# First attention of a two-layer graph network: where the halves of a finished unit are added, on VectorE or on GpSimd

## The reference, cut to what matters

```python
wh = (x @ weight).reshape(n, NHEADS, OUT_FEATURES)
awh_i = (wh * linear_i).sum(axis=2)
awh_j = (wh * linear_j).sum(axis=2)
e = leaky_relu(awh_i[:, None, :] + awh_j[None, :, :], negative_slope=0.2)
e = e + ((1.0 - adj) * NEG_INF)[:, :, None]
a = softmax(e, axis=1)
out = einsum('ijh,jhf->ihf', a, wh)
```

## Time and profile before

| | us |
|---|---|
| median of 3 runs (4261.85 to 4263.58) | 4261.97 |
| the profiled execution, its device time | 4264.08 |
| its span, first to last instruction | 4260.6 |
| gat, from about 495 to 1493 us of the span | 998 |
| in gat: PE busy / DVE busy / ACT busy / POOL busy | 960.0 / 979.1 / 948.6 / 5.6 |

### The profile page before, as it was taken

One profiled execution on the slowest core, in us unless ns is written; L12 is line 12 of the kernel. 1 busy time (PEld: TensorE's weight loads), 2 busy tenths in 40 slices (PEclk: granted clock), 3 DMA queues, 4 the chain that ended last, 5 costly groups with the idle time before them and its releaser, 6 DMA issues. The chain is left out here.

```text
span 4260.6 us, 104547 instructions
## 1 busy us (share of the span) xinstructions
PE 3773.0 (89%) x42884; PEld 2512.9 (59%) x42884; DVE 3499.7 (82%) x6039; ACT 3344.7 (79%) x4233; POOL 439.5 (10%) x635
## 2 busy tenths in 40 slices
PE   7981399999999969919999999999999999999977
PEld 4540399999999924405555555555555555555533
DVE  6655699999999977638888888888888888888734
ACT  3433699999999822209999999999999999999932
POOL 1211100000000000020120201201112011120000
PEclk9995699999999979959999999999999999999989
DMA  9988855555554377662453534444445354353133
GB/s 347 392 287 210 242 175 170 184 188 189 189 188 164 121 206 238 209 174 71 116 138 90 142 95 119 133 101 131 107 108 138 93 142 109 95 143 93 45 111 138
DMA packets 364121, 674.35 MB, mean 158 GB/s; under 512 B 79584, under 2 KB 239408, under 8 KB 326784
## 3 DMA queue, kind: packets, MB, share of 16 engines
q1 hardware_dynamic: 296448, 574.83, 45.3%
q0 software_dynamic: 24064, 84.37, 6.5%
q10 hardware_dynamic: 43136, 8.53, 1.0%
HBM read 524.43 MB, written 143.20 MB: 157 GB/s over the span
## 5 line engine op out<-in xcount | busy, mean ns | idle before, releaser
L1230 DVE CUSTOM_DVE_ANT_0 m_junk<-m_rough,m_rows 128x1024 bf16<-128x1024 f32 x1024 | 1253.5, 1224 | 287.8 <-PE m_rough L1097 226.3
L1179 ACT ACTIVATE m_scores<-m_strip 128x1024 f32<-128x1024 fp8e4 x1024 | 1052.3, 1028 | 102.4 <-POOL m_strip L1028 37.9
L1193 ACT ACTIVATE m_whole<-m_scores 128x1024 int32<-128x1024 f32 x1024 | 1038.0, 1014 | 35.9 <-PE m_scores L1130 25.5
L630 PE MATMUL g_acc<-g_vals,g_pos 128*128 128x130 f16 x8192 | 956.4, 218 | 48.6 <-DVE g_neg L585 48.6
L547 ACT ACTIVATE g_step<-g_arow,k_steep 128x512 fp8e4<-128x512 f32 x1536 | 948.6, 707 | 40.2 <-DVE g_pos L578 37.2
L630 PE MATMUL g_acc<-g_vals,g_neg 128*128 128x130 f16 x8192 | 955.8, 221 | 0.0
L1111 PE MATMUL m_acc<-m_v,m_halves 128*128 128x129 f16 (+1 forms) x16384 | 897.1, 208 | 45.2 <-ACT m_got L1156 45.2
L1111 PEld LDWEIGHTS m_acc<-m_v,m_halves 128*128 128x128 f16 x16384 | 751.0, 98 | 279.8 <-issue 186.5
L630 PEld LDWEIGHTS g_acc<-g_vals,g_pos 128*128 128x128 fp8e4 x8192 | 801.9, 98 | 59.5 <-DVE g_neg L585 37.1
L1125 PE MATMUL m_scores<-m_qA,m_kA 128*128 128x512 f16 x2048 | 780.7, 381 | 5.7 <-ACT m_scores L1179 5.6
L630 PEld LDWEIGHTS g_acc<-g_vals,g_neg 128*128 128x128 fp8e4 x8192 | 784.9, 96 | 0.0
(11 more groups left out here) (161 smaller groups left out, 3005.2 us busy)
## 6 DMA issues: line engine op xcount, KB each, us to landing
g_vals<-scr_gat_v SPq DMA_DIRECT2D x128, 1040.0 KB, 5.1
m_v<-scr_v SPq DMA_DIRECT2D x64, 1032.0 KB, 7.9
a_stage<-in_adj SPq DMA_DIRECT2D x64, 1024.0 KB, 9.3
m_kA<-scr_k_hi SPq DMA_DIRECT2D x128, 512.0 KB, 6.2
scr_row_mask<-a_rowm SPq DMA_DIRECT2D x64, 512.0 KB, 7.6
m_kB<-scr_k_lo SPq DMA_DIRECT2D x64, 512.0 KB, 5.4
m_rows<-scr_row_mask POOLq DMA_DIRECT2D x64, 512.0 KB, 7.3
scr_gat_v<-a_early POOLq DMA_DIRECT2D x32, 520.0 KB, 6.9
```

What stands on the lines that cost most here:

```text
L630: mm = pe.matmul(acc[:, b, it, lo:hi], edges[:, n % RING, t, rows], vals[:, b, 4 * j + t, lo:hi], start=j == 0 and t == 0 and lo == 0, sto ...
L1179: nc.scalar.activation(scores[:, n % 2], strip[:, 2 * st:2 * st + 2, :].rearrange("p t i -> p (t i)"), ACT.Copy, bias=-BIG, scale=BIG / ED ...
L1193: nc.scalar.activation(whole[:, st % 2], scores[:, st % 2], ACT.Exp, scale=0.125).then_inc(exped, 1)
L1230: nc.vector.tensor_tensor_reduce(out=junk[:, n % 2], in0=rough[:].rearrange("p a m -> p (a m)"), in1=rows[:, n % TC, n // TC * WIDE:(n // ...
```

## The change

VectorE keeps only line 592 of `evacuate`. The three additions move to GpSimd, which now runs a function `join(u)` for each unit: it waits for `evac`, adds the halves (`part`, which raises the new semaphore `parted`), waits for its own `parted`, and adds `num` and `k.den`. VectorE may overwrite `scaled` for unit u only when GpSimd has read it for unit u - 1: one new wait, for `parted`, ahead of line 592. GpSimd waits for its own `den_made` before it overwrites `part`. The stage ends when GpSimd's last DMA has landed and its last `k.den` is written.

```diff
-        chain, evac, num_ready, passed = (s.sem(n) for n in ("chain", "evac", "num_ready", "passed"))
+        evac, parted, den_made, num_ready, passed = (s.sem(n) for n in ("evac", "parted", "den_made", "num_ready", "passed"))
...
                 dve.wait_ge(multiplied, QUADS * (u + 1))
+                if u > 0:
+                    dve.wait_ge(parted, u)
                 nc.vector.tensor_tensor(scaled[:], acc[:, b, :, 0:2 * VG].rearrange("p q (z v) -> p q z v", z=2),
                                         k.row_factors[:, c * TC:(c + 1) * TC, h, :].unsqueeze(3).to_broadcast([P, TC, 2, VG]),
                                         ALU.mult).then_inc(evac, 1)
-                dve.wait_ge(evac, u + 1)
-                link(nc.vector.tensor_tensor(part[:], scaled[:, :, :, 0:F + 1], scaled[:, :, :, F + 1:VG], ALU.add))
-                if h == 0 and c >= 2:
-                    dve.wait_ge(num_out[c % 2], 16 * (c // 2))
-                link(nc.vector.tensor_tensor(num[:, c % 2, :, h, :], part[:, :, 0, 0:F], part[:, :, 1, 0:F], ALU.add))
-                if h == H - 1:
-                    dve.sem_inc(num_ready, 1)
-                nc.vector.tensor_tensor(k.den[:, c * TC:(c + 1) * TC, h:h + 1], part[:, :, 0, F:F + 1], part[:, :, 1, F:F + 1], ALU.add)
...
         def _(pool):
+            def join(u):
+                c, h = u // H, u % H
+                pool.wait_ge(evac, u + 1)
+                if u > 0:
+                    pool.wait_ge(den_made, u)
+                nc.gpsimd.tensor_tensor(part[:], scaled[:, :, :, 0:F + 1], scaled[:, :, :, F + 1:VG], ALU.add).then_inc(parted, 1)
+                pool.wait_ge(parted, u + 1)
+                if h == 0 and c >= 2:
+                    pool.wait_ge(num_out[c % 2], 16 * (c // 2))
+                nc.gpsimd.tensor_tensor(num[:, c % 2, :, h, :], part[:, :, 0, 0:F], part[:, :, 1, 0:F], ALU.add).then_inc(num_ready, 1)
+                nc.gpsimd.tensor_tensor(k.den[:, c * TC:(c + 1) * TC, h:h + 1], part[:, :, 0, F:F + 1], part[:, :, 1, F:F + 1],
+                                        ALU.add).then_inc(den_made, 1)
+
             for c in range(C):
-                pool.wait_ge(num_ready, c + 1)
+                for h in range(H):
+                    join(c * H + h)
+                pool.wait_ge(num_ready, H * (c + 1))
                 pool.dma_start(y_v[:, c * TC:(c + 1) * TC, :], num[:, c % 2].rearrange("p t h f -> p t (h f)")).then_inc(num_out[c % 2], 16)
```

More of the change, by code:

```diff
@@ L552, in _ @@
         def _(dve):
-            link = Chain(dve, chain)
             def words(ap):
@@ L640, in _ @@
                 pool.wait_ge(num_out[b], 16 * C // 2)
+            pool.wait_ge(den_made, U)
 def project_heads(nc, k, x, Wks, Wqs, Wvs, scr):
```

## The result

The changed kernel takes 4251.31 us (median of 8 runs, 4245.9 to 4255.44), the kernel before beside it 4262.65 (8 runs): a ratio of 0.9974, interval 0.9963 to 0.9985. It is 11 us faster, and was forecast 10 us slower. The time lies in the stated range, on the wrong side of no change. The profiled execution has a span of 4249.8 us.

A forecast was written before the change was run, and what follows sets the result against it. VectorE was taken to bound the stage; 13.95 us left plus 1.57 of holds gave 15.52 a unit, 0.14 more, +9 us over 63 units; with +0.7 at the end, +10 to 4272 us, range 4236 to 4290.

The forecast's parts named there:

- What bounds the stage: In the one stage touched, VectorE sets the pace: 15.38 us a unit, of which 12.80 eight quads and 2.58 reading out.
- The floor of 14.94 by TensorE: With VectorE free of charge, a unit would still take 14.94 us by TensorE, capping the gain at 28 us.
- the rival in which the two engines don't meet: Fourth rival, chance 0.05: GpSimd and VectorE never hold each other, so the gain is the cap, 28 us, 4235 us.
- What leaves VectorE: Reading out shrinks from 2.58 to 1.15 us a unit, 1.43 less; VectorE alone would need 13.95 us.
- That the engines shut each other out, and whom: In a quad, all VectorE instructions share something with GpSimd and can be held; only line 592 doesn't.
- the open direction: Two-input VectorE instruction behind a GpSimd one: no row showed its price, between nothing and full hold; full hold was taken.
- The first rival: Chance 0.2: a GpSimd read doesn't hold two-input VectorE instructions; only line 565 is held, unit 14.99 us, 4238 us.
- the second: Rival, chance 0.15: each exchange also loses instruction overlap; unit 15.94 us, +35 us, 4298 us.
- the third: Rival, chance 0.05: GpSimd gets in only when VectorE rests at line 592; unit 15.19 us, 4251 us.
- What a hold costs: VectorE loses 1.14 us to `part`, 0.59 to `num`, 0.06 to `den`, less 0.15: 1.64, or 1.49 by lower slope; middle 1.57.
- what comes back: After each of three holds VectorE regains 0.05 us, read from line 1255; 0.15 us a unit.
- The end of the stage: Last unit's join has nothing beside it; its DMA comes 2.2 us after line 592 instead of 1.55: +0.7 us.

## Why the prediction was wrong, point by point

- **What bounds the stage.** Right: VectorE. The pace read from a single unit, 15.38, was 0.03 below the mean of 15.41, which is 2 us in 62 units: the steps at the end of a block were longer, and the change took that away as well. The floor of 14.94 by TensorE was too high; it is 14.80. That didn't enter the sum, but the rival in which the two engines don't meet should have been 10 us lower.
- **What leaves VectorE.** Right: the mask starts 1.15 us behind line 592, and VectorE's own work is 13.95 us.
- **That the engines shut each other out, and whom.** Right, with the open direction: a two-input instruction is held in full (line 583 ends 0.55 us after `num`). The first rival (two-input instructions not held), the second (dearer exchanges), the third (GpSimd last) and the fourth (no meeting) are all excluded by the trace of the changed kernel. One premise was weaker than it was told: of the two GpSimd instructions in the earlier trace rows, line 1046 ends (1960.75) as line 1230 starts (1960.73), so only line 1048 ran beside it. That line 592 shares nothing was right even so: `part` ran beside it at 0.97 us past its wait, and line 592 took 1.24.
- **What a hold costs. This is the step that failed**, as a size in two of its terms. First, the price of the additions: I took 1.23 us for `part` and 0.70 for `num`, the middle of two slopes of the earlier trace rows; they take 1.12 and 0.64. The rows were of additions whose inputs lie 64 apart, or were in place; those of the change lie 65 apart. For `num` the runs show that this is the reason (0.64, and 0.09 more at 64 or 128 apart); for `part` no other distance was run. The holds were 0.98 and 0.50, where the sum had 1.09 and 0.57. Second, what comes back: I took 0.05 us for each hold from line 1255. Line 563 ended 0.28 us after GpSimd, and it ends 0.39 after a VectorE predecessor, so 0.11 came back. Measured from start to start, line 563 lost 1.26 - 0.39 = 0.87 (the sum had 1.04) and line 583 1.05 - 0.60 = 0.45 (0.52). VectorE lost 1.32 us a unit instead of 1.57.
- **What that did to the sign.** 1.43 leaves and 1.32 comes: 0.11 less a unit and not 0.14 more. Of the 0.25 between, 0.18 is the price of the additions, 0.06 what line 563 got back, and 0.01 `den`, which held nothing; the price alone would have left the forecast at 0.04 less, no change that a measurement could tell. The 0.25, over 63 units, is 16 of the 21 us between forecast and result; the mean of the pace is 2 more, and the rest is within the interval. The forecast was the small difference of two large terms, with ends from the two slopes that were both too high: 1.9 ns a number, the lower, where (1.12 - 0.21) / 516 = 1.76 was measured. The page that the forecast cited (the Trainium skill, "GPSIMD Engine Reference", section "Elementwise — side-by-side cycle accounting") would give 2.17, an estimate; no form that ran here was so dear (the dearest, 0.73 us for 256 numbers, gives 2.1).
- **The end of the stage.** Right: from the end of line 592 (1484.22) to the DMA (1486.43) 2.2 us, where the earlier trace rows have 1.55.

## What to carry to other kernels

An addition moved from VectorE to GpSimd isn't taken off VectorE if its neighbours there read SBUF: count the time from start to start that it had on VectorE against the part of GpSimd's duration that holds the neighbour, one by one. Here `num` and `den` were a gain (0.34 us a unit) and `part` on top of them a loss (0.18). `part` was free beside a VectorE instruction that has one of its inputs in PSUM: a second buffer and another release of the join made the gain 0.95% instead of 0.26%. And take the price of an addition from a row with the same distance between its inputs: where a forecast is the small difference of two large terms (here 0.14 us a unit), an error of 0.18 in one of them turns its sign.

## What was not expected of the hardware

- A GpSimd addition of 256 float32 numbers took 0.72 to 0.73 us at each distance between its two inputs that was a multiple of 4 numbers (16 bytes; 64, 256, 260 and more), and 0.64 at 65, 257 and 258 numbers. In the form of `num` the 0.09 us shows up in the VectorE instruction that it holds. In place it took 0.68; what sets that price wasn't run.
- GpSimd doesn't get its turn at the next boundary between two VectorE instructions: behind step and behind neg it was passed over, for up to 2.41 us in all, and let in ahead of the one-input line 563. After a hold, and when it asked beside line 592, it got in ahead of a mask too.
- A GpSimd fill and a two-input VectorE instruction ran side by side at 0.53 and 0.68 us, neither stretched.
